# Where the median search of the next image is cut in: turning's groups, the back transform, the convolutions' taps

## The reference, cut to what matters

```python
# x: 16 x 64 x 128 x 128
q_in = jnp.quantile(x.reshape(B, C, -1), 0.5, axis=-1)      # a median per image and channel
x = x + relu(-q_in)[:, :, None, None]
y = upfirdn2d(x, lpf, up=2, ...); y = maximum(y, 0); y = upfirdn2d(y, lpf, down=2)
...
spec = rfft2(x); mag = abs(spec)
gate = sigmoid(w2 @ gelu(w1 @ mag))
xf = x + irfft2(spec * gate)                                # the back transform
q = xf @ q_w + q_b
k, v from conv(xf, 8x8, stride 8) and conv(xf, 16x16, stride 16), layernorm, linear, 3x3 depthwise
out = softmax(q k^T / 4) v @ proj_w + proj_b + x
```

## Time and profile before

| what | value |
|---|---|
| median of 3 runs | 12244.59 us (12242.68 to 12251.3) |
| the profiled execution's own time | 12252.08 us |
| its span | 12250.4 us |
| mean granted clock of TensorE | 0.915 of 2.4 GHz |
| busy share PE, DVE, ACT, POOL | 87%, 73%, 59%, 22% |

### The profile page before, as it was taken

How to read it: one execution, slowest core, us unless ns; L and a number is a source line. 1 busy time by engine, 2 the same in 40 slices (tenths; PEclk the granted TensorE clock), 3 DMA queues, 4 the chain that set the end, 5 groups by cost and what they waited for, 6 DMA issues and landing times. The chain is left out here.

```text
span 12250.4 us, 196159 instructions
## 1 busy us (share of the span) xinstructions
PE 10635.3 (87%) x71137; PEld 5483.3 (45%) x71137; DVE 8883.1 (73%) x15501; ACT 7242.7 (59%) x12109; POOL 2713.5 (22%) x4368
## 2 busy tenths in 40 slices
PE   2898898988989899898988989889898898989989
PEld 1544435344453444535445354443534435344453
DVE  6777677776777777777676777767777677777777
ACT  4656465664646646466564665646566464664646
POOL 1212213122131221312223121221312213122130
PEclk9899898998989899898998989989899898989989
DMA  2021120212212022130211202112021221202213
GB/s 61 19 43 45 42 63 20 53 34 47 58 29 56 22 52 53 32 60 22 50 49 38 67 19 45 44 43 62 22 52 33 48 57 29 56 22 52 53 32 73
DMA packets 176568, 537.63 MB, mean 44 GB/s; under 512 B 64872, under 2 KB 87400, under 8 KB 154032
## 3 DMA queue, kind: packets, MB, share of 16 engines
q1 hardware_dynamic: 175664, 525.24, 19.0%
HBM read 232.43 MB, written 71.30 MB: 25 GB/s over the span
## 5 line engine op out<-in xcount | busy, mean ns | idle before, releaser
L948 DVE TENSOR_REDUCE R<-ps 128x2 f32<-128x640 f32 x4096 | 3195.1, 818 | 920.8 <-PE ps L685 910.6
L1156 ACT ACTIVATE R<-ps 128x512 f32<-128x512 f32 x5120 | 2820.5, 594 | 644.8 <-PE ps L706 620.1
L249 ACT ACTIVATE R<-R,st 128x1475 bf16<-128x1475 f32 x1326 | 2018.1, 1522 | 787.8 <-DVE st L318 761.0
L306 DVE TENSOR_SCALAR_CACHE_REDUCE R<-R,st 128x1255 bf16<-128x1255 f32 x1326 | 2011.7, 1517 | 22.0
L685 PE MATMUL ps<-KST,R 96*128 96x320 bf16 x8192 | 1877.1, 312 | 67.8 <-DVE R L948 57.5
L731 PE MATMUL ps<-R 128*32 128x512 f32 x12288 | 1635.3, 605 | 38.2 <-DVE Wk L902 33.1
L706 PE MATMUL ps<-R,KST 104*128 104x512 bf16 x4096 | 1576.4, 387 | 21.3 <-ACT R L1156 20.5
L685 PEld LDWEIGHTS ps<-KST,R 96*128 96x128 bf16 x8192 | 761.4, 100 | 830.6 <-DVE R L948 303.2
L1240 POOL CAST R<-Wk 128x512 bf16<-128x512 f32 x256 | 283.4, 1107 | 2932.2 <-DVE Wk L902 2932.2
L706 PEld LDWEIGHTS ps<-R,KST 104*128 104x128 bf16 x4096 | 395.7, 97 | 709.0 <-ACT R L1156 461.6
L204 PE MATMUL ps<-st,cst 128*128 128x6 f32 x884 | 191.9, 289 | 591.1 <-DVE R L306 217.2
(11 more groups left out here) (206 smaller groups left out, 19620.1 us busy)
## 6 DMA issues: line engine op xcount, KB each, us to landing
R<-R SPq DMA_DIRECT2D x3072, 64.0 KB, 2.4
R<-xh_in SPq DMA_DIRECT2D x136, 512.0 KB, 4.4
out_dram<-Z SPq DMA_DIRECT2D x68, 1024.0 KB, 3.9
R<-xa_in SPq DMA_DIRECT2D x36, 1024.0 KB, 11.3
R<-xb_in SPq DMA_DIRECT2D x36, 1024.0 KB, 12.0
R<-sr_in SPq DMA_DIRECT2D x32, 1024.0 KB, 4.8
R<-sr_in SPq DMA_DIRECT2D x16, 2016.0 KB, 9.7
R<-sr_in SPq DMA_DIRECT2D x16, 1056.0 KB
```

The lines of the kernel that those rows point to most:

```text
L249: e.activation(junka[:, 0:o2 - o1], xc[:, o1:o2], ACT.Sign, bias=mid, scale=-1.0, accum_out=cnt[:, NP + i:NP + i + 1]).then_inc(md_ca, 1)
L306: e.tensor_scalar(junk[:, 0:o1 - o0], xc[:, o0:o1], mid, None, ALU.is_le, ALU.add, accum_out=cnt[:, i:i + 1]).then_inc(md_cv, 1)
L948: e.tensor_reduce(MX[(4 * u + s4) % 2][:, blk_, h0:h0 + 2], ps[:, 2 + 2 * bq:4 + 2 * bq, 0:320], axis=AX.X, op=ALU.max).then_inc(mx, 1)
L1156: e.activation(PB[:, t % 2, w, :], ps[:, w % 2, :], ACT.Exp).then_inc(ex, 1)
```

## The change

The scanning places leave the gate except for two, in the first loop (groups 3 and 6). The other sixteen go into the back transform, one in each of the rounds 0 to 15; PE's place stands behind the third of its four groups of matmuls. The filter's places go behind them: DVE has eight in the turning (one after each of its copies), 25 after the addition to Z of `stage(0, 0)` and one after each of the next three; PE has five in the turning, 26 in the first convolution (one behind each tap from the seventh on) and five in the second; POOL has all it needs ahead of the query stages up to the fifth filter round, and 25 more behind `stage(0, 0)`. MF and TF move from R5, which QH and QM now need, into Wk. In the last five of the 26 steps DVE counts 0.36 of the columns and ACT 0.64, in the others 0.46 and 0.54 as before. SyncE waits for filter round 8 before the first unit's loads and for round 16 before the second's, no longer for the end.

```diff
-MIDS = [a + int(0.46 * (b - a)) for a, b in zip(CUTS, CUTS[1:])]
+MIDS = [[a + int((0.46 if k < 21 else 0.36) * (b - a)) for a, b in zip(CUTS, CUTS[1:])] for k in range(STEPS)]
-        MF = [R5[:, 256 * i:256 * i + 256].bitcast(BF16) for i in range(3)]
-        TF = [R5[:, 768 + 512 * i:1280 + 512 * i] for i in range(2)]
+        MF = [W[:, o:o + 256].bitcast(BF16) for o in (0, 256, 2624)]
+        TF = [W[:, 512 + 512 * i:1024 + 512 * i] for i in range(2)]
...
 # PE: gate's first loop; its two other loops lose their slots
-                slot(1 if grp % 3 else 0)
+                slot(1 if grp in (3, 6) else 0)
 # PE: back transform
+            slot(1)
+                        slot(1 if i == 2 and m < 15 else 0)
-                slot(2 if n < 17 else 1)
 # PE: turning, second convolution, first convolution
+                slot(1 if grp in (0, 6, 10, 12, 14) else 0)
+                    slot(1 if x in (3, 7, 27, 47, 95) else 0)
-                slot(1 if n in (2, 5, 8) else 0)
+                slot(1 if n > 5 else 0)
-            for _ in med:
-                pass
...
 # DVE: gate
-                slot(1 if grp % 3 else 0)
-            for grp in range(12):
-                slot(1)
+                slot(1 if grp in (3, 6) else 0)
 # DVE: back transform, turning, stages
-                slot(1 if n < 17 else 0)
+                slot(1 if n < 16 else 0)
-                slot(1 if n < 16 else 0)
-            for _ in med:
-                pass
+                slot(1)
+                slot((25, 1, 1, 1)[j])
...
 # ACT: gate, back transform
-            slot(6)
+            slot(2)
-                slot(1 if grp % 3 else 0)
+                slot(1 if n < 16 else 0)
 # POOL
             slot(18)
-            for _ in med:
-                pass
+            slot(8)
...
+                slot((25, 1, 1, 1)[j])
 # SP
-            e.wait_ge(md_end, 1)
+            e.wait_ge(md_mm, 8)
             load_unit(e, 0)
+            e.wait_ge(md_mm, 16)
             load_unit(e, 1)
```

More of the change, by code:

```diff
@@ L27 @@
 CUTS = [HALF * i // NP for i in range(NP + 1)]
-MIDS = [a + int(0.46 * (b - a)) for a, b in zip(CUTS, CUTS[1:])]
-SIGNED = sum(b - m for m, b in zip(MIDS, CUTS[1:]))
-FEWER = 2.0 * (RANK - SIGNED)
+MIDS = [[a + int((0.46 if k < 21 else 0.36) * (b - a)) for a, b in zip(CUTS, CUTS[1:])] for k in range(STEPS)]
+FEWER = [2.0 * (RANK - sum(b - m for m, b in zip(ms, CUTS[1:]))) for ms in MIDS]
 P = C // 2
@@ L208, in pe_median @@
                 yield
[L209 to L217, removed]
+            for i in range(16):
+                e.wait_ge(md_ta, i + 1)
+                b7.free(e)
+                for q in range(4):
+                    j = q % 2
+                    op = e.matmul(ps[64 * j:64 * j + 64, 7, 336:464], lhsT=pairb[:, :], rhs=MF[i % 3][:, 128 * q:128 * q + 128],
+                                  start=i == 0 and q < 2, stop=i == 15 and q > 1)
+                op.then_inc(md_fs, 1)
                 yield
@@ L245, in act_median @@
                 for i in range(NP):
-                    o1, o2 = MIDS[i], CUTS[i + 1]
+                    o1, o2 = MIDS[k][i], CUTS[i + 1]
                     if k or i:
@@ L264, in pool_median @@
                     e.wait_ge(md_raise, k)
-                e.tensor_scalar(lift, gg, FEWER, BIG, ALU.is_lt, ALU.mult).then_inc(md_lift, 1)
+                e.tensor_scalar(lift, gg, FEWER[k], BIG, ALU.is_lt, ALU.mult).then_inc(md_lift, 1)
                 e.wait_ge(md_lift, 2 * k + 1)
@@ L302, in dve_median @@
                 for i in range(NP):
-                    o0, o1 = CUTS[i], MIDS[i]
+                    o0, o1 = CUTS[i], MIDS[k][i]
                     if k or i:
@@ L315, in dve_median @@
                     e.wait_ge(md_g, 2 + k)
-                    e.tensor_scalar(uu, gg, FEWER, hs[:, k + 1:k + 2], ALU.is_lt, ALU.mult).then_inc(md_got, 1)
+                    e.tensor_scalar(uu, gg, FEWER[k], hs[:, k + 1:k + 2], ALU.is_lt, ALU.mult).then_inc(md_got, 1)
                     e.wait_ge(md_got, 2 + k)
@@ L574, in tensor @@
                 op.then_inc(g_ps, 1)
-                slot(1 if grp % 3 else 0)
-            for n in range(18):
+            slot(1)
+            for n in range(1, 18):
                 m = n - 1
-                if 0 <= m < 16:
+                if m < 16:
                     k = m % 2
```

## The result

| | median | all runs | profiled execution |
|---|---|---|---|
| before | 12245.57 us | 12242.68 to 12251.3 (4) | 12252.08, span 12250.4, clock 0.915 |
| after | 12027.47 us | 12015.28 to 12047.03 (4) | 12015.28, span 12013.6, clock 0.935 |

The change makes the kernel faster: ratio 0.9823, interval 0.9806 to 0.984, 218 us. The forecast was 11975, with 11895 to 12095 as its range; the time lies in the range, 52 us above the point. The lines of the code shift by a few: L306 is now L304, L546 L544, L557 L555, L570 L567, L878 L873, L884 L879, L613 L610, L892 L886, L644 L643, L633 L631, L910 L903.

What follows compares the result with a forecast made beforehand. The search was taken to bound the gate, PE the back transform and convolutions. Per image -24.0 - 1.4 + 3.1 + 5.2 = -17.1, x 16 = -274, +4 gives -270: 11975 us, range 11895 to 12095.

Steps and rivals of the forecast that it cites:

- The gate, -24.0: Gate: with search places cut from 18 to 2, it shortens from 50.5 us by 24.0 per image (bounds -22.6, -25.2).
- T+27.9: Gate: first product's start, counted from the first turning matmul T, if the clock stays at 1.2 GHz throughout.
- T+25.3: Gate: first product's start, counted from the first turning matmul T, if the clock is 2.4 GHz for the w2 loop.
- The back transform, -1.4: Back transform: 14 rounds at 3.17 us add 1.8, a shorter beginning saves 3.2; -1.4 per image (bounds -3.2, +3.5).
- the beginning gets shorter: Start of the back transform: 9.3 us falls to 6.1, -3.2 at full clock or -1.5 at low clock.
- Rival C: Rival, chance 0.14: back transform's every third round, DVE waits for PE's count; 3.5 us a round, +4.6 per image, 12048 us.
- The turning, +3.1: Turning: filter rounds 0 to 4 join DVE's copies, 10.6 us against 7.5; +3.1 per image (bounds +2, +5).
- The convolutions, +5.2: Convolutions: beside the filter they end at S+43.3 against S+38.1, PE waiting 2.2 us; +5.2 per image (bounds +3.5, +7).
- The queues: Behind the convolutions: SyncE's last split moves 4.7 us later, less than PE's 5.2, so no further wait.
- B: Rival, chance 0.17: low clock in gate (+1.4), first two back-transform rounds (+1.7) and second convolution (+3); 12073 us.
- D: Rival, chance 0.04: PE's gaps in turning and between taps keep the clock down; convolutions +13 per image, 12454 us.
- E: Rival, chance 0.03: no change; B and Rival C together with convolutions and turning at upper bounds, -2.7 per image, 12205 us.

Runs made afterwards that it cites:

- experiment 4: Kernel after, with the w2 loop's first eight groups of matmuls contracting 128 rows against a zero-padded copy of w2: 11969.21 us, ratio 0.9776.
- experiment 5: Kernel after, with DVE copying only four of the 16 groups in the turning and ACT twelve: 12017.94 us, ratio 0.9816.
- experiment 7: Kernel after, with DVE's first addition to Z (2.28 us) behind the 25 filter places, not before them: 12076.9 us, ratio 0.9859.
- the quickest kernel: Kernel after, with 128-row w2 loop, ACT copying more, Z addition behind filter places, PE's small steps later, count behind fourth group: 11910.08 us, ratio 0.9723.
- experiment 1: Kernel after, with the search back in the gate (18 places, all steps split 0.46), so only the filter moves: 12336.9 us, ratio 1.0075.

## Why the prediction was right, and where it was off

*The gate, -24.0.* Measured -23.6 (50.52 to 26.91). PE's turnings and the w2 loop set it, ACT's two scans are hidden. The bounds were for the clock low throughout, T+27.9, or up in the loop, T+25.3; it is high when the loop begins and low through most of it, the reverse of the forecast's rise. The parts were less good than the sum. In the third image (27.5 us) the w1 matmuls end at T+13.0 (1974.78), not T+14.6, and from there to the first product it takes 14.5 us and not 11.9, with PE waiting 1.56 us for the first sigmoid where it was to work "without a pause". An error of 1.6 us and one of 2.6 cancel in part.

*The back transform, -1.4.* Measured +1.4, and **this is the term that was mis-sized**, by the part that said "the beginning gets shorter": 9.3 to 6.1 us at full clock, 1.5 less if the clock is still low. It is 9.3, as before. The forecast had the clock up a little into the w2 loop, since PE "works without a pause" from there. It is at 0.50 for the first 7.8 to 9.5 us of the back transform in eleven images; in the other five it rises 3.7 us in, and "first" is 7.9 or 8.0. The low clock alone costs 2.8 us of the image, as the images of experiment 4 show (9.4 or 9.5 for 6.6), not 1.7. The *size* of a round was right, 3.18 us for 3.17, but for another reason than the forecast's, and so by luck. It had PE at 3.05 and DVE at 3.15 and chose DVE. DVE's own work is 2.96 a round (9.55 less 0.66 idle, by three), and PE's is 3.18: 2.95, and 0.69 for the count every third round, where 0.18 a round had been set aside. Rival C's wait is there too, 0.39 of DVE for the count, but it doesn't set the round, and a round comes to 3.18 with it and not to 3.5.

*The turning, +3.1.* Measured +2.9, with DVE as the bound: experiment 5 took 2.7 us of it by taking four copies from DVE.

*The convolutions, +5.2.* Measured +5.1, but +1.8 in the first and +3.3 in the second, where the working had +0.4 and +4.8. With S the end of DVE's last copy (2055.66), POOL's addition 12 ends at S+18.7, not S+18.0, since the cycle is 1.57 beside the taps, not 1.52, and starts later. Mark 14 is counted at S+20.65 (2076.31), and behind it stand another 1.2 us of taps, where the working had 0.1 to 0.9. So PE comes later to the serial step and waits 0.93 us, not 2.2. The later the one, the shorter the other. Still, the sum is closer than it deserved: the working's own terms from S+27.2 on (0.7, 11.7, 2.1 and 0.9) give S+42.6 and not S+43.3. The rule of the Trainium skill that was weighed there ("SBUF — State Buffer", "Who interferes with whom") holds in this trace too: mark and addition follow each other, 0.36 and 1.20. Beside DVE's addition of 2048 columns a cast of POOL takes 2.60 us, and 0.61 without it (experiment 7).

*The queues.* SyncE's last loads delay nothing; the stages "kv" and "rows" are as before.

*The sum.* -23.6 + 1.4 + 2.9 + 5.1 is -14.2, and the search's own stage "up" is 0.9 shorter, about what it varies by from kernel to kernel (166.9 to 168.0 us); that gives -15.1 for the forecast's -17.1. Times 16 that is 32 us of the 52 between point and median. The first median took +2.9 for +4. The rest lies between the medians and the profiled executions: the profiled one of after is 12 us below its median, that of before some 7 above.

*The rivals.* B was priced as three things. The beginning of the back transform at low clock happened, and cost nearly twice its 1.7 us. The pause in the second convolution brought no fall of the clock in the profiled execution of this kernel. Experiment 7, with 3.14 us, shows B's mechanism in every image, at some 1.3 us and not 3; four other kernels show it behind the same 0.93 us in 30 of 64 images. B's median of 12073 is far from 12027. C's wait is there and its size isn't. D would need the clock at 0.5 in the convolutions; it is at 1.00. E is excluded by the interval.

## What to carry to other kernels

Put filler work by the engine it needs, and count what it adds to the engine that is the bound, however small: the split of the scans between DVE and ACT cost nothing here, while two small matmuls on PE cost 0.69 us each time, and their place and that of one 2.28 us addition on DVE moved some 15 and 49 us. When a round gets the size that you forecast, look which engine has no idle time in it before you call the reason right. Of a stretch at low clock, ask what its matmuls look like before you fill its pauses. Edits that move waits can only be valued together: the addition's new place lost 49 us by itself and belonged to the quickest kernel once the step behind it stood later.

## What was not expected of the hardware

- PE was busy for 8.00 of 8.00 us in matmuls mostly of 32 contracted rows, and its clock fell from 2.4 to 1.2 GHz and stayed there. With 128 rows in the same loop it kept 2.4 GHz at 4.22 busy of 5.00. The busy share of the records doesn't tell whether the clock holds.
- A wait of 3.14 us between taps, at full clock before it, brought 1.2 GHz in sixteen of sixteen images, for 6.8 us in fifteen of them. One of 0.93 us at the same place brought it for 3.4 us in 30 of 112 images of seven kernels, from none of sixteen in after to eleven of sixteen in experiment 1. What decides it is open.
- Once up in the w2 loop, the clock still fell at the gate's end in ten of sixteen images of one execution of the same code. The ten differ from the six by when the clock had fallen ahead of the gate, by a microsecond or so. Why is open.
